# Flamingo gated cross-attention block: 36 identity transposes on TensorE at the start, and the mask sums moved behind the fifth projection of queries

## The reference, cut to what matters

```
x = x + tanh(g_xattn) * xattn(layernorm(x), ctx, mask)     # x: 2 x 512 x 256, ctx: 2 x 1024 x 256
x = x + tanh(g_ffn)   * experts(layernorm(x))              # 8 experts, the largest gate decides

xattn: q = layernorm(x) @ Wq    (256 -> 1024 = 16 heads x 64)
       k, v = ctx @ Wk, ctx @ Wv
       dots = where(mask, -max, q k^T / 8);  softmax;  @ v;  @ Wo + bo
```

## Time and profile before

| | |
|---|---|
| median of 3 runs | 241.98 us (241.69, 241.98, 244.35) |
| the profiled execution | 242.49 us, span 240.7 us |
| PE busy | 217.7 us, 90% of the span |
| DVE, ACT, POOL busy | 56%, 47%, 38% |
| PE in the chain that ended last | 68% |

### The profile page before, as it was taken

One profiled execution on the slowest core, in us unless ns is written; L12 is line 12 of the kernel. 1 busy time (PEld: TensorE's weight loads), 2 busy tenths in 40 slices (PEclk: granted clock), 3 DMA queues, 4 the chain that ended last, 5 costly groups with the idle time before them and its releaser, 6 DMA issues.

```text
span 240.7 us, 4102 instructions
## 1 busy us (share of the span) xinstructions
PE 217.7 (90%) x1316; PEld 145.8 (61%) x1316; DVE 134.3 (56%) x537; ACT 112.5 (47%) x386; POOL 90.5 (38%) x96
## 2 busy tenths in 40 slices
PE   0499999999999999999999799999999999959960
PEld 0334394456555544488894356565568899948950
DVE  0797424678878722325227777788883435345520
ACT  2101443877887721301234868778844034525420
POOL 5000710555544591000001657755483000776450
PEclk9999999999999999999999999999999999999995
DMA  3990658999990000091000100240000000235011
GB/s 113 365 394 26 183 234 252 331 317 313 233 316 13 0 3 1 0 297 52 3 1 0 46 3 22 62 143 0 0 3 1 3 0 0 82 112 162 31 49 30
DMA packets 21250, 25.24 MB, mean 105 GB/s; under 512 B 1875, under 2 KB 19805, under 8 KB 21088
## 3 DMA queue, kind: packets, MB, share of 16 engines
q1 hardware_dynamic: 19200, 22.58, 30.4%
q0 software_dynamic: 1152, 2.12, 2.6%
q10 hardware_dynamic: 864, 0.15, 0.3%
HBM read 14.21 MB, written 11.68 MB: 108 GB/s over the span
## 4 chain that ended last, share of the span: by engine, by line
PE 68%; issue 12%; DMA 6%; DVE 5%; POOL 4%; ACT 3%; POOLq 0%; DVEq 0%
PE s_bank L1491 11%; PE s_bank L1531 10%; PE bank L1560 8%; PE bank L1563 7%; PE bank L1450 6%; PE bank L1544 5%; PE s_bank L1588 4%; PE s_bank L1776 3%; PE bank L1545 3%; PE bank L1548 3%; DMA oT<-sorted_rows 2%; PE bank L1571 2%; PE bank L1787 2%; DMA rows<-in_x_dram 2%; POOL sorted_rows L537 2%
## 5 line engine op out<-in xcount | busy, mean ns | idle before, releaser
L563 POOL TENSOR_TENSOR probs<-probs,r_col 128x768 f32<-128x768 f32 x32 | 46.9, 1466 | 86.5 <-DVE r_col L1148 86.5
L717 ACT ACTIVATE probs<-probs,negm_run 128x192 f32<-128x192 f32 x128 | 57.1, 448 | 19.5 <-DVE negm_run L1173 19.5
L1173 DVE CUSTOM_DVE_ANT_0 probs<-s_bank,maskneg 128x192 f32<-128x192 f32 x128 | 39.5, 348 | 8.6 <-PE s_bank L1531 8.6
L1491 PE MATMUL s_bank<-xnT,wq_sb 128*128 128x512 f32 x64 | 31.7, 644 | 1.2 <-ACT xnT L670 0.6
L1182 DVE COPY pT<-bank 128x512 f32<-128x512 f32 x32 | 22.1, 691 | 13.6 <-PE bank L1545 13.6
L1531 PE MATMUL s_bank<-k_sb,q_sb 64*128 64x192 f32 x256 | 29.5, 349 | 0.0
L1450 PE MATMUL bank<-wo_sb,oT 128*128 128x256 f32 x128 | 28.7, 380 | 0.0
L1450 PEld LDWEIGHTS bank<-wo_sb,oT 128*128 128x128 f32 x128 | 23.9, 190 | 3.9 <-issue 0.9
L1531 PEld LDWEIGHTS s_bank<-k_sb,q_sb 64*128 64x128 f32 x256 | 20.0, 186 | 9.0 <-issue 7.9
L717 ACT ACTIVATION_READ_ACCUMULATOR probs<-probs,negm_run 128x1 f32 x128 | 24.1, 188 | 0.0
L1491 PEld LDWEIGHTS s_bank<-xnT,wq_sb 128*128 128x128 f32 x64 | 12.6, 206 | 16.4 <-issue 15.0
(11 more groups left out here) (141 smaller groups left out, 288.5 us busy)
## 6 DMA issues: line engine op xcount, KB each, us to landing
sorted_rows<-empty_row SPq DMA_DIRECT2D x8, 1040.0 KB, 13.3
oT<-in_L_ffn_W_dram SPq DMA_DIRECT2D x1, 2048.0 KB, 17.6
q_sb<-in_L_ffn_W_dram SPq DMA_DIRECT2D x1, 2048.0 KB, 8.4
oT<-sorted_rows SPq DMA_DIRECT2D x1, 1040.0 KB, 6.6
oT<-sorted_rows SPq DMA_DIRECT2D x8, 130.0 KB, 2.2
rows<-in_x_dram SPq DMA_DIRECT2D x2, 512.0 KB, 7.8
wq_sb<-in_L_xattn_Wq_dram SPq DMA_DIRECT2D x1, 1024.0 KB, 8.3
mask_sb<-in_mask_BxSxS_bk_dram SPq DMA_DIRECT2D x2, 512.0 KB, 9.9
```

The costliest lines, as they stand in the source:

```text
L563: nc.gpsimd.tensor_tensor(part, part, r_col[:, u % PB].rearrange("p i h -> p (i h)") .unsqueeze(2).broadcast_to([P, 4, keys]), ALU.mult).t ...
L717: last = nc.scalar.activation(window_part(u, i, h), window_part(u, i, h), ACT.Exp, bias=negm_run[at], scale=-1.0, accum_out=l_run[at])
L1173: nc.vector.tensor_tensor_reduce(window_part(u, i, h), s_bank[u % 2][:, h, i * CK:i * CK + WK], maskneg[:, q, 0:WK], -SCALE, LARGEST, ALU. ...
L1491: last = nc.tensor.matmul(bank[m % 4], wq_sb[:, c, m * P:(m + 1) * P], xnT[:, c, b * N:(b + 1) * N], start=(c == 0), stop=(c == DC - 1))
```

## The change

It has three edits. TensorE, once the identity is there, transposes it 36 times into a PSUM bank (bank 7) that nothing reads before it is written again. On TensorE the sums over the mask, with the b1 transposes behind them, stand behind block 4 of the queries and no longer behind block 2. On DVE the copy of block 3 stands ahead of the variance of batch 1 and no longer behind it.

```
+    WARM = 36
...
             dve.wait_ge(s_x[1], 16)
+            take_q(0, 3)
             variance(range(QT, TT))
-            take_q(0, 3)
             norm(QT, TT, xn, ln_ready)
...
             pe.wait_ge(ident_ready, E + 3)
 
+
+            for _ in range(WARM):
+                nc.tensor.transpose(bank[7][:, 0:P], ident[:], ident[:])
+
             def xn_transposes(b):
...
             for m in range(M):
                 project_q(0, m)
-                if m == 2:
+                if m == 4:
                     visit_sums()
                     pe.wait_ge(s_b1, 16)
                     for ic in range(IC):
```

## The result

The changed kernel takes 243.83 us (median of 20 runs, 243.05 to 247.33) against 242.81 us (20 runs, 241.68 to 245.32): ratio **1.0047, 95% interval 1.0027 to 1.0066**, 1.1 us slower. I had forecast 246.0 us, 3.5 us over the profiled execution. The sign was right and the size three times too large. On three other comparisons, further down, the same kernel came out at 1.009, 1.013 and 1.014, so the size itself needed explaining (the runs' spread doesn't do it: the intervals of 1.0047 and 1.0128 don't touch).

What follows compares the result with a forecast made beforehand. PE, busy 90% of the span, was taken as the bound, with DVE and ACT setting the pace between early query blocks and block 6. 242.49 + 0.84 (chain) + 2.7 (clock lost in the hole) = 246.0 us; range 243.0 to 249.3.

Steps and rivals of the forecast that it cites:

- The term for the hole: TensorE from block 6: clock lost in the idle time, then 5.4 us at half pace, costing 2.7 us.
- From there the work of TensorE is the same, and it is TensorE that the chain follows: From block 6 to the end: TensorE's work unchanged, so block 6's 0.84 us delay passes on.
- The order of events at the front: Start to block 6: transposes, block 0 at 10.98, sums at 19.62, copy of block 3, variance, block 6 at 26.60.
- The 36 transposes: TensorE's start: hidden behind the wait for x, cost zero (bounds 0 to 0.7 us), clock raised before block 0.
- The rival that they don't raise it: TensorE's start: transposes don't raise the clock, block 0 at 12.1 at half pace; 247.1 to 249.8 us, chance 0.25.
- the sentence of the Trainium skill: Transposes don't count as activity as matmuls do, and the fast clock doesn't engage for them; by it 247 to 250 us.
- a start a microsecond later: TensorE's start: beginning the transposes 1 us later moves their end about half a microsecond, still near 8.9.
- The chain: Sums to block 6: 6.30 us plus 0.68 for the copy, sums 0.16 later; block 6 0.84 us later.
- The hole: TensorE ahead of block 6: idle 4.7 us instead of 0.52, long enough to lose the clock.
- the sum: Whole kernel: 242.49 + 0.84 + 2.7 = 246.0 us, with nothing added for the late stage.
- The rival that the clock is kept: Hole ahead of block 6 doesn't drop the clock, or gives it back at once; 243.3 us, chance 0.15.

Runs made afterwards that it cites:

- a0: The changed kernel again with no edit, timed against the kernel before: ratio 1.0128.
- d3: The changed kernel a fourth time, no edit, on a chip without the late stand, against the kernel before: ratio 1.0090.
- c3: The changed kernel a third time, no edit, on a chip with the late stand, against the kernel before: ratio 1.0140.
- a3: The changed kernel plus 34 transposes of the identity behind block 5, filling the hole; ratio to the kernel before 1.0020.
- b2: The changed kernel with the copy of block 3 back behind the variance of batch 1; ratio to the kernel before 1.0166.
- groups b and d: Two sets of follow-up runs on one chip without the late stand, each timed against the kernel before; ratios from 0.9791 to 1.0253.
- a2: The kernel before plus the 36 transposes alone, sums and copy of block 3 left in place; ratio to the kernel before 0.9931.
- d1: The changed kernel without the 36 transposes, both moves kept, a third time; ratio to the kernel before 1.0253.
- c2: The kernel before plus the 36 transposes alone, a second time, on a chip with the late stand; ratio 0.9977.

## Why the prediction was right and wrong

Two steps failed. The term for the hole, 2.7 us, was too large: 1.8 us on average were measured. And the step "From there the work of TensorE is the same, and it is TensorE that the chain follows" put the late stage at nothing, where the changed kernel got 1.3 us back. The order of events at the front came as forecast.

*The 36 transposes.* Right. They take 5.7 to 7.0 us, raise the clock before x is there, and cost nothing; block 0 starts at 10.6 to 10.8 in all profiles but the one with the late x (10.98 forecast; x came 0.1 to 0.3 us earlier) and from there it is 8.75 us to the sums (8.64 forecast). The rival that they don't raise it is refuted by every profile with them. So is, for this form, the sentence of the Trainium skill ("TensorE: Matmul & The Clock Gate", Part 4) that I weighed: float32 transposes of 128x128 back to back brought TensorE to 2.4 GHz after 3.2 to 5.8 us, with no matmul before them. The trace calls them MATMUL and doesn't say in which mode they ran. One slip in the working: by the rule used there a start a microsecond later would move the end by a whole microsecond, past 8.89, not by half. TensorE started at 1.80, so nothing hung on it.

*The chain.* Right. From the sums to block 6 it is 6.90 us in a0, d3 and c3 against 6.30 before, and the sums come at 19.4 to 19.5. Against the earlier trace rows block 6 is 0.6 us later with x 0.3 us earlier, so 0.9, against the 0.84 of the forecast. The kernel before, though, is itself better than its first profile (block 6 at 24.94 and 25.12 in the two others), as its clock rose earlier there; against those the front costs 1.2 to 1.4 us. That early rise was not in the forecast.

*The hole.* The mechanism was right and is shown from both sides: it is 4.55 us long in all four profiles of the changed kernel, the clock falls in it or within a microsecond behind it in each, and a3 gets the loss back by filling it. The term was mis-sized: I took 2.7 us with a rise that takes as long as at the start. Blocks 6 and 7 lost 1.70, 1.52, 1.70 and 2.15 us in the four profiles (5.40, 5.22, 5.40 and 5.85 less 3.70), mean 1.8, as the rise came 3.1 to 4.4 us after block 6 began, not 5.4; b2 reached 2.8. It scatters from one execution to the next: in d3's ten runs the three with a mean clock of 0.985 to 0.987 took 243.1 to 243.5 us and the seven with 0.972 to 0.980 took 243.7 to 245.1.

*What the sum lacked.* The step "from there the work of TensorE is the same" holds to 208 us: the lag of each profile's matmuls behind those of the kernel before stays constant to 0.02 us from 32 to 208 us. But the same work doesn't get the same code loads. On chips without the late stand the first read of sorted rows is 1.2 to 1.7 us shorter in every kernel with the 36 added pairs, which makes the late stage 1.3 us shorter (1.65 in d3) and hides about half of the loss. With both, on the chip of groups b and d, by the two profiles: + 1.2 (block 6 at 26.28 against 25.12) + 2.15 (clock) - 1.65 (late stage) = 1.7 us, 241.9 against 240.0 in span (1.9). For the 20 runs the front's 0.9 to 1.4, plus 1.8, less 1.3, make 1.4 to 1.9, measured 1.1; where the rest went is not shown, as the one profile of that comparison is the one with the late x. On the two chips with the stand nothing is given back, and the kernel is 3.1 and 3.4 us slower than before: there the forecast's 3.5 is close, and its two terms as measured, 0.9 to 1.4 and 1.8, make 2.7 to 3.2.

*The rival that the clock is kept* gives nearly the measured time, 243.3, and is still false: its cause was not seen in any profile. Two errors of opposite effect met there, and that 243.83 lies inside the stated range, near its lower end of 243.0, is luck for the same reason.

*Left open.* What TensorE and ACT wait for in the late stand, and whether the kernel before has it too. I didn't profile the kernel before on those chips. Three things speak for it: it takes 6 to 9 us longer there; the mean granted clock of its runs is 0.961 to 0.975 there and 0.981 to 0.991 on the chip without the stand; and c4, which is the kernel before but for 36 small transposes, has the stand and 10 us at half clock behind it.

## What to carry to other kernels

Before moving work to an engine that a change makes faster, follow what each later step waits for: here blocks 3 to 5 were the cover of a 6.3 us chain through DVE and ACT, and the cure was one line on ACT, a square root and a table load put behind two copies that were ready, not a place for the sums. With the transposes it gave 0.979 to 0.982, of which 1.3 us, about a quarter, are the moved load of code. An idle time on TensorE that loses the clock costs its length and then again up to half of what follows, until the clock is back; the same hole filled with transposes that nobody reads cost only its length. And when a late stage moves by a microsecond after an edit at the start, look for loads of code in it before crediting the edit.

## What the runs showed of the hardware that was not expected

- Transposes count for the clock. 36 of 128x128 raised it each time (ten profiles). Of the waits behind dense work, 3.95 to 4.55 us lost the clock each time. Near 2 us it went either way: 1.86 us in a2, 1.93 in d1 and 2.42 in the first profile of the changed kernel were followed by a fallen clock, 1.88 us in c2 and 2.29 in the kernel before were not.
- One load of 16 KB of code (1.4 us on the queue) lengthened a read of sorted rows from 2.1 to 3.7 us, its last sixteenth waiting for the load's end, and 36 pairs of instructions 200 us earlier in the program decided it, large (128x128) or small (8x128, 4.0 us for all).
- The same kernel took 242 or 249 to 251 us by chip, with a stand of 4 to 6 us at one place of the program and a low clock behind it.
